# The start of a fused kernel: the first weights' later pieces issued by ScalarE, their first piece in two transfers, and seven idle matmuls instead of eight

## The reference

```python
g = sigmoid(xn @ gate_w.T + gate_b); u_g = xn * g            # recurrent branch s
s = c * G * cumsum(b * u_g / G) + (d + d_lr) * u_g           # G = cumprod(tanh(a)), d_lr from the mean of u_g
h = silu(silu(xn @ w1.T) @ w3.T) @ w2.T                      # feed-forward branch
out[indices_k] += gates * h                                  # top-2 of a softmax over 8 routes
return x + s * silu(out)
```

## Time and profile before

| | before |
|---|---|
| median of 3 runs | 730.24 us (730.24 to 730.76) |
| profiled execution, its own time | 730.16 us |
| its span, first to last instruction | 728.3 us |
| TensorE busy | 723.7 us, 99% of the span |
| granted TensorE clock over the span | 1.000 |
| DMA, mean over the span | 174 GB/s |

### The profile page before, as it was taken

One profiled execution on the slowest core, in us unless ns is written; L12 is line 12 of the kernel. 1 busy time (PEld: TensorE's weight loads), 2 busy tenths in 40 slices (PEclk: granted clock), 3 DMA queues, 4 the chain that ended last, 5 costly groups with the idle time before them and its releaser, 6 DMA issues.

```text
span 728.3 us, 10078 instructions
## 1 busy us (share of the span) xinstructions
PE 723.7 (99%) x4194; PEld 601.8 (83%) x4194; DVE 517.9 (71%) x508; ACT 357.7 (49%) x447; POOL 21.3 (3%) x34
## 2 busy tenths in 40 slices
PE   9999999999999999999999999999999999999998
PEld 8888888888888888888888888888888888888887
DVE  5988467758675786699989987357588756885522
ACT  6648849255755675354924553324244441463221
POOL 0000000002010010000000000000000000000000
PEclk9999999999999999999999999999999999999999
DMA  8616835678365847869676803341138103300140
GB/s 336 252 58 230 296 154 197 243 265 289 116 234 168 295 142 265 289 217 332 218 274 230 317 3 144 129 161 51 39 125 307 58 1 145 144 2 1 55 181 4
DMA packets 31118, 126.81 MB, mean 174 GB/s; under 512 B 4760, under 2 KB 4952, under 8 KB 23904
## 3 DMA queue, kind: packets, MB, share of 16 engines
q1 hardware_dynamic: 21824, 109.37, 42.2%
q10 hardware_dynamic: 9248, 16.80, 6.3%
HBM read 105.08 MB, written 37.78 MB: 196 GB/s over the span
## 4 chain that ended last, share of the span: by engine, by line
PE 99%; DVE 0%; ACT 0%; issue 0%
PE main L949 31%; PE main L950 31%; PE main L951 31%; PE lgp L1028 2%; PE lgp L1041 1%; PE spare L1041 1%; PE spare L956 1%; PE main L978 0%; PE main L981 0%; PE main L984 0%; PE lgp L1055 0%; PE main L1055 0%; DVE tail L1102 0%; ACT u L939 0%; DVE lg L1437 0%
## 5 line engine op out<-in xcount | busy, mean ns | idle before, releaser
L1102 DVE TENSOR_TENSOR s<-s,main 128x512 f32<-128x512 f32 x72 | 48.6, 682 | 63.2 <-PE main L951 63.2
L1102 DVE TENSOR_TENSOR u<-u,main 128x512 f32<-128x512 f32 x36 | 24.3, 683 | 35.2 <-PE main L951 35.2
L805 ACT ACTIVATE s<-main 128x512 f32<-128x512 f32 x36 | 20.9, 593 | 44.4 <-PE main L951 21.9
L830 ACT ACTIVATE rows<-rows 128x512 f32<-128x512 f32 x16 | 10.0, 632 | 65.4 <-DVE rows L1102 65.4
L1102 DVE TENSOR_TENSOR u<-s,main 128x512 f32<-128x512 f32 x32 | 21.6, 684 | 24.8 <-PE main L951 24.8
L751 ACT ACTIVATE rows<-rows,nm 128x1024 f32<-128x1024 f32 x32 | 36.9, 1153 | 1.0
L749 ACT ACTIVATE rows<-rows 128x1024 f32<-128x1024 f32 x32 | 33.6, 1049 | 5.4 <-DMA rows<-x 4.3
L830 ACT ACTIVATE s<-s 128x512 f32<-128x512 f32 x24 | 15.0, 630 | 42.3 <-DVE s L1102 42.3
L830 ACT ACTIVATE u<-u 128x512 f32<-128x512 f32 x24 | 15.1, 628 | 29.3 <-DVE u L1102 29.3
L1102 DVE TENSOR_TENSOR rows<-s,main 128x512 f32<-128x512 f32 x16 | 10.8, 685 | 21.8 <-PE main L951 21.8
L950 PE MATMUL main<-x7r,wh2r 128*128 128x512 f32 x48 | 18.7, 389 | 0.0
(11 more groups left out here) (656 smaller groups left out, 2374.3 us busy)
## 6 DMA issues: line engine op xcount, KB each, us to landing
rows<-x SPq DMA_DIRECT2D x32, 512.0 KB, 4.7
out<-x SPq DMA_DIRECT2D x31, 512.0 KB, 10.2
H_d<-u ACTq DMA_DIRECT2D x32, 256.0 KB, 4.6
H_d<-s ACTq DMA_DIRECT2D x16, 256.0 KB, 5.0
bc<-mv_d SPq DMA_DIRECT2D x8, 512.0 KB, 4.3
rows<-w SPq DMA_DIRECT2D x8, 512.0 KB, 5.2
rows<-xh_d SPq DMA_DIRECT2D x16, 256.0 KB, 5.3
w2f<-w2T SPq DMA_DIRECT2D x2, 2048.0 KB, 10.0
```

Of the source, the lines that this page charges most:

```text
L805: eng.activation(s1[:, j, :], bk, ACT.Copy).then_inc(s_pa, 1)
L830: eng.activation(c, c, ACT.Silu).then_inc(s_sl, 1)
L1102: return eng.tensor_tensor(o, a, b, op)
```

## The change

`first_weights` on SyncE now issues only the pieces of block "c" and, for block "a", piece 0 as two transfers of 256 columns (128 KB each), the first of which raises a new semaphore `s_wd`, the second the old one. Pieces 1 to 3 of block "a" are issued by ScalarE directly behind its one-column Silu. ScalarE waits for `s_wd` ahead of the copy of the first half and for the old semaphore ahead of the second. One idle matmul of eight goes.

```diff
+        s_wd = sem("s_wd")
@@ SyncE
             for b in "ac":
                 for k in range(PIECES[b]):
                     first_block(b, k)
-                    first_weights(b, k)
+                    if (b, k) == ("a", 0):
+                        for e in range(2):
+                            of = slice(2 * P * e, 2 * P * (e + 1))
+                            eng.dma_start(w_from(0, 0)[:, 0, of], w11[0][:, of]).then_inc(s_w0["a"][0] if e else s_wd, 16)
+                    elif b == "c":
+                        first_weights(b, k)
@@ ScalarE
             on.wait_ge(s_po, 1)
             eng.activation(nm[:, :], mhalf[:, 0:1], ACT.Silu)
+            for k in range(1, PIECES["a"]):
+                eng.dma_start(part(w_from(0, 0), "a", k), w11[k]).then_inc(s_w0["a"][k], 16)
@@ ScalarE, first_weights(b, k)
                 p = "ac".index(b)
+                if (b, k) == ("a", 0):
+                    on.wait_ge(s_wd, 16)
+                    eng.activation(w_r(0, 0)[:, 0, 0:2 * P], w_from(0, 0)[:, 0, 0:2 * P], ACT.Copy).then_inc(s_wc, 1)
                 on.wait_ge(s_w0[b][k], 16)
                 if (b, k) == ("a", 0):
-                    eng.activation(w_r(0, 0)[:, 0, 0:2 * P], w_from(0, 0)[:, 0, 0:2 * P], ACT.Copy).then_inc(s_wc, 1)
                     eng.activation(w_r(0, 0)[:, 0, 2 * P:HT], w_from(0, 0)[:, 0, 2 * P:HT], ACT.Copy).then_inc(s_wh0, 1)
                     return
@@ TensorE
-            warm(spare, 8)
+            warm(spare, 7)
```

## The result

The changed kernel is slower: 733.09 us median (731.23 to 734.56, 13 runs) against 730.71 us (730.24 to 731.19, 13 runs); the ratio is 1.0034, 95% interval 1.0027 to 1.0042. That is 2.4 us where 0.1 less was forecast and 731.1 was the end of the range. The scatter grew too, from 1.0 to 3.3 us, and the thirteen times fall into three groups: four from 731.23 to 731.54, four from 732.68 to 733.49, five from 734.29 to 734.56. The profiled execution is one of the quick ones: 731.23 us, with a span of 729.4.

A forecast was written before the change was run, and what follows sets the result against it. TensorE bounds the kernel, so only its start could move the end. With k = 1 at 7.4 instead of 7.53 us, the sum was 730.16 - 0.15 + 0.08 = 730.1 us, range 729.7 to 731.1.

The forecast's parts named there:

- What bounds the kernel: Whole kernel: TensorE is busy 723.7 of 728.3 us, so early edits move the end only by moving its hole-free stream.
- ScalarE ends its small Silu at 2.23 ... so 2.25, 2.7 and 3.15: ScalarE's three weights' issues: they go out after the Silu, end at 3.6 us and cost ScalarE nothing.
- Rival 2: ScalarE's pieces start at 0.9, 1.35 and 1.8, delaying the first data: +0.2 to +1.0 us, middle 730.8; chance 10%.
- Lands near 5.1 ... the first transfer of a queue that had been empty: Weights' piece 1, issued by ScalarE: with 2.8 us of transfer it lands near 5.1 instead of 6.74 us.
- I take 4.6: Landing of the first weights' piece's second half: 4.6 us, within 4.47 to 6.07, so tile j = 2 starts at 5.1.
- rival 3: Second half as slow as the earlier third transfer: lands 5.2 to 6.07, +0.4 to +1.35 us, 731.1; chance 9%.
- I take 5.9: Landing of x piece 1, now SyncE's fourth transfer: 5.9 us, making k = 1 ready at 7.4.
- rival 1: x piece 1 shares the DMA engines and loses its lead: k = 1 ready at 8.19, +0.66 us, 730.9; chance 18%.
- The hole's price: Hole between idle and real matmuls: might keep the clock low through k = 0, +2.7 us, 732.9; chance 3%.
- rival 5: The hole delays the clock's rise beyond k = 0, whose twelve matmuls take twice 0.23: +2.7 us, 732.9; chance 3%.
- One idle matmul less: TensorE's start: two loads of 0.21 us go, so the next load could begin at 3.98 instead of 4.41.
- The start at 4.26: First real load: first half lands near 3.73, copied by 4.15, so it starts at 4.26 instead of 4.60 us.

The follow-up runs named there:

- the late issues: The changed kernel, but ScalarE waits for the end of its Silu before issuing the weights' pieces 1 to 3: 732.01 us, ratio 1.0019.
- the split alone: The kernel before with the weights' first piece in two transfers, all issued by SyncE, eight idle matmuls: 730.91 us, ratio 1.0005.
- the issues alone: The kernel before with the weights' pieces 1 to 3 issued by ScalarE, first piece whole, eight idle matmuls: 731.31 us, ratio 1.0015.

## Why the prediction was wrong

**What bounds the kernel** held: the end moves by what the first load of the regular order moves, within 0.2 us in every trace (own time less that load's start is 717.09 to 717.26 in all fourteen).

**"ScalarE ends its small Silu at 2.23 ... so 2.25, 2.7 and 3.15"** is the first step that failed. The issues went out at 0.87 to 2.23. Only one row was there for it, an issue beside running activations, and it pointed this way; I set the forecast by the end of the Silu, with no row for that. The rule on the sequencer that the prediction quotes from the Trainium skill (Advanced Engine Details and Errata, Sequencer Loop) pointed the same way; the trace agrees, with an issue at 0.87 inside a table load of 0.74 to 2.02. Rival 2 had this mechanism, at 10% and a middle price of 0.6; the trace says 1.07 for all late data together, at full clock. Put right, this step does not save the forecast: with the issues held back to 2.27 the kernel still took 732.01.

**"Lands near 5.1 ... the first transfer of a queue that had been empty"** failed too. Issued behind the Silu, that piece took 5.9 us and landed at 8.2. An empty queue was no free lane here.
The Trainium skill (DMA: Bandwidth & Descriptors, Issuing engines are not separate DMA queues) says that transfers run on the same 16 DMA engines whichever engine started them, and that starting them on several engines saves only the issuing engine's time. The pair of pieces issued together at 0.73, landing 0.8 and 0.4 us later than before, agrees.

**"I take 4.6"** for the second half was a choice at the wrong end of its bounds (4.47 to 6.07). It landed near 6.0 in the changed kernel, 5.8 with the late issues, 5.5 with the split alone: the third transfer of SyncE is late at 128 KB as at 256. The row for it was there, 4.4 us for the third. This is rival 3 (9%): it had k = 1 at 7.9 to 8.9, and the quick trace has 8.67.

**"I take 5.9"** for x piece 1 was the step that the forecast's last sum stood on, and it failed as well. The piece landed at 7.3 in the changed kernel, 7.4 with the late issues, 7.6 with the issues alone and 6.7 with the split alone. The data of k = 1 was ready at 8.66 instead of 7.4, so the late second half is not needed to explain k = 1 at 8.67. This is rival 1 (18%), whose sign was a landing later than 6.07 and whose price, k = 1 at 8.19, was too low. The work that the prediction gave the DMA engines in their idle stretch was done (369 instead of 229 GB/s) and did not bring x piece 1 sooner.

**The hole's price** is the largest term, 1.3 to 1.5 of 2.4 us in the median, and I gave it 3%. The prediction had the mechanism (rival 5) and an estimate that the idle matmuls run at the lower level, then let the column of the granted clock speak against it. The estimate was right: in the trace of ScalarE's issues alone the idle loads go from 0.21 to 0.11 us apart when the clock rises, and in the kernel before it rose at 4.82. Shown: five idle matmuls instead of eight cost 1.75 us with no data late; eleven in the changed kernel give back 1.45; four loads take 1.61 us behind the hole in the slow traces and 0.88 otherwise. That this is the clock at 1.2 instead of 2.4 GHz is shown by the ratio of these paces (0.43 to 0.23 us a load) together with the clock's records, which begin where the pace changes. A hole that comes behind the rise costs only itself: with the split alone 1.17 us ahead of j = 2, and the loads behind it 0.23 apart. Why the rise came at 4.52, 4.95 and 9.63 in three executions of one kernel is open. Its price for one execution is not a fixed 2.7 us: k = 0 from j = 2 on took 2.18 us in the quick execution, 3.71 in the slow one and 4.01 (6.25 to 10.26) with the late issue, so between nothing and 1.8 us in the traces.

**One idle matmul less** was taken as harmless where it opens no hole. Alone it is (730.52 against 730.50). With the data 1 us late the medians differ, 733.09 against 731.87 us (two sessions whose kernels before agree within 0.05), but not clearly beyond the scatter.

**The start at 4.26** was right where its condition held: 4.31 with ScalarE's issues held back, 4.41 with the split alone and eight idle matmuls.

So of 2.4 us about 1.1 are late data by the quick trace (0.9 by the median of the kernel with eleven idle matmuls), and the remaining 1.3 to 1.5 are put down to the slow pace behind the hole; this split of the median is an estimate, since only three executions of the changed kernel were traced. The two parts of the data's share are not additive to the tenth: the split alone +0.4 and the issues alone +0.8 in the median, the former no change that can be told.

## What to carry to other kernels

A second issuing engine did not speed the first piece here; it put pieces that are needed late ahead of those that are needed now. Issue in the order of need, and count an engine's own issue as going out as soon as its sequencer reaches it. Size the idle matmuls for the latest arrival of the data, not for the usual one: an extra one cost nothing here, while a hole ahead of the clock's rise cost up to 1.8 us in the traces. Its price shows only where the data leaves no slack behind it: with seven idle matmuls in the kernel before the slow loads were there and cost nothing.

## What the runs showed that I had not expected

With no transfer of ScalarE in flight early, SyncE's third transfer landed 3.7 to 5.2 us after its issue whether it held 256 or 128 KB, the first two 2.5 to 3.0 us; with ScalarE's issues from 0.87 the third took 4.2 to 5.9 and the first two 2.8 to 3.7. Why the third is late is not settled. The column of the granted clock reads 1.00 from the first instruction, also where loads stand 0.43 us apart: at the start of a program the pace of the loads, or the time at which the clock's records begin, is the better clock. The kernel with a hole in TensorE's work there scattered over 3.3 us, and its three traces have the rise of the clock 5 us apart.
